# Result rows of the sorted products scattered to their tokens' places, and loaded in the third stage with plain transfers

## The reference

```
h  = concat(token_table[ids], cat_table[ids])                       # [64, 128, 256]
x1 = layernorm(h);  q, k, v = split(x1 @ W_qkv + b_qkv)              # 16 heads of 16
h  = h + linear_attention(elu(q) + 1, elu(k) + 1, v)                 # over each row of 128 tokens
x2 = layernorm(h)
rw = softmax over the experts with a positive gated logit of x2      # [tokens, 16]
q  = einsum('btc,ech,bte->bth', x2, q_proj, rw)   # and k, v likewise; 256 -> 128
ao = causal softmax(q k^T / sqrt(128)) v                             # over each row of 128 tokens
out = h + einsum('bth,ehc,bte->btc', ao, o_proj, rw)                 # 128 -> 256
```

## Time and profile before

| | us |
|---|---|
| median of three runs | 1116.49 |
| the profiled execution | 1116.51 |
| its span (first to last instruction) | 1114.8 |

### The profile page before, as it was taken

One profiled execution on the slowest core, in us unless ns is written; L12 is line 12 of the kernel. 1 busy time (PEld: TensorE's weight loads), 2 busy tenths in 40 slices (PEclk: granted clock), 3 DMA queues, 4 the chain that ended last, 5 costly groups with the idle time before them and its releaser, 6 DMA issues.

```text
span 1114.8 us, 23702 instructions
## 1 busy us (share of the span) xinstructions
PE 971.9 (87%) x6831; PEld 894.7 (80%) x6831; DVE 873.4 (78%) x2889; ACT 586.3 (53%) x1569; POOL 700.2 (63%) x924
## 2 busy tenths in 40 slices
PE   0788888878888872899999969999999999999998
PEld 0677777767777761889999859999999999999997
DVE  2578888788888875655555439999999999999998
ACT  1465666566566640444444435555555555555554
POOL 6667666566666667500000068888888888888885
PEclk9999999999999995999999969999999999999999
DMA  6464334433333324698888633333333333333331
GB/s 202 129 202 145 119 105 143 133 122 121 111 108 114 105 77 156 216 289 276 257 256 259 226 93 92 93 96 95 96 96 91 94 93 96 89 95 91 93 95 34
DMA packets 132325, 150.56 MB, mean 135 GB/s; under 512 B 14708, under 2 KB 119650, under 8 KB 132196
## 3 DMA queue, kind: packets, MB, share of 16 engines
q1 hardware_dynamic: 112964, 97.59, 28.2%
q0 software_dynamic: 18080, 50.36, 15.3%
q10 hardware_dynamic: 1152, 1.05, 0.3%
HBM read 83.79 MB, written 78.88 MB: 146 GB/s over the span
## 4 chain that ended last, share of the span: by engine, by line
PE 51%; DVE 24%; issue 9%; POOL 5%; DMA 4%; ACT 4%; SPq 1%; another core or an unknown queue 1%; POOLq 0%; DVEq 0%; ACTq 0%
PE bank L1429 11%; PE bank L1431 10%; PE bank L1430 10%; PE bank L1436 7%; PE bank L1460 5%; DVE w_attn L1412 5%; DVE qk_e L1366 3%; DVE row_x L1406 3%; DVE x L1366 3%; PE bank L1515 3%; DMA h<-in_L_tok_special_table,ids 2%; PE bank L1456 1%; ACT x L854 1%; PE bank L1631 1%; PE bank L1639 1%
## 5 line engine op out<-in xcount | busy, mean ns | idle before, releaser
L1429 PE MATMUL bank<-wo_hi,split_lo 128*128 128x256 f32 x1024 | 304.6, 297 | 10.0 <-DVE x L1366 4.4
L1431 PE MATMUL bank<-wo_hi,split_hi 128*128 128x256 f32 x1024 | 288.8, 282 | 0.0
L1430 PE MATMUL bank<-wo_lo,split_hi 128*128 128x256 f32 x1024 | 288.4, 282 | 0.0
L1429 PEld LDWEIGHTS bank<-wo_hi,split_lo 128*128 128x128 f32 x1024 | 194.0, 189 | 23.3 <-DVE qk_e L1366 11.2
L1430 PEld LDWEIGHTS bank<-wo_lo,split_hi 128*128 128x128 f32 x1024 | 194.2, 190 | 0.0
L1431 PEld LDWEIGHTS bank<-wo_hi,split_hi 128*128 128x128 f32 x1024 | 193.6, 189 | 0.0
L938 ACT ACTIVATE h<-bank,rwo 128x256 f32<-128x256 f32 x256 | 107.3, 470 | 115.2 <-PE bank L1431 111.4
L816 POOL DMA_INDIRECT row_y<-sorted_y,pair_now x128 | 124.1, 970 | 31.3 <-issue 21.3
L809 POOL COPY pair_now<-pair_at 128x2 uint32<-128x2 uint32 x64 | 11.7, 183 | 179.2 <-SPq L599 179.1
L1267 DVE TENSOR_TENSOR split_lo<-bank,split_hi 128x256 fp32r<-128x256 f32 x144 | 60.8, 422 | 68.7 <-ACT split_hi L900 67.4
L1366 DVE SCALAR_TENSOR_TENSOR qk_e<-bank,rwo,qk_e 128x256 f32<-128x256 f32 x256 | 108.6, 473 | 3.7 <-PE bank L1431 3.0
(11 more groups left out here) (228 smaller groups left out, 2675.4 us busy)
## 6 DMA issues: line engine op xcount, KB each, us to landing
sorted_y<-row_y SPq DMA_DIRECT2D x36, 384.0 KB, 3.1
sorted_y<-w_attn SPq DMA_DIRECT2D x36, 384.0 KB, 3.1
row_x<-sorted_x SPq DMA_DIRECT2D x72, 128.0 KB, 2.9
h_rows<-h SPq DMA_DIRECT2D x64, 128.0 KB
row_x<-h_rows SPq DMA_DIRECT2D x64, 128.0 KB, 2.2
out_h<-row_x SPq DMA_DIRECT2D x64, 128.0 KB, 1.7
embed_table<-in_L_tok_token_table SPq DMA_DIRECT2D x10, 625.0 KB
embed_table<-in_L_tok_special_table SPq DMA_DIRECT2D x10, 623.0 KB
```

The source lines that it names most:

```text
L1429: pe.matmul(ps, left[1][c], right[0][c], start=(c == 0), stop=False)
L1430: pe.matmul(ps, left[0][c], right[1][c], start=False, stop=False)
L1431: last = pe.matmul(ps, left[0][c], right[0][c], start=False, stop=(c == n - 1))
```

## The change

What is stored from the second stage isn't in sorted order any more. Each sorted row carries two marks behind its 256 values: its expert, and twice its token's number. So a row of `sorted_x` has 258 values (1032 bytes), and so have the buffers `x2` (12 now, 10 before), the zero rows and the loads of the second stage. Zero rows carry expert 0 and a token number beyond all tokens. For each pair tile VectorE forms the rows' destinations: twice the token number, plus one where the mark differs from the expert of the tile (the second choice of that token). GpSimd scatters each product to that row of `token_y`, 144 indirect DMAs with a bounds check that drops zero rows. The third stage loads a token tile's two rows of each token with one plain DMA from SyncE's queue, where GpSimd gathered them. The row arithmetic on GpSimd at the start of the second stage and three links of VectorE's table chain are gone.

```diff
@@ first stage: marks
+                slots = slice(first % N_X2, first % N_X2 + n)
+                dve.tensor_copy(marks[:, slots, C], top_at[:, tiles, 0])
...
                 for t in scatters_at(i.c):
-                    quad_done(pool, "position_index", group_of(t))
+                    g = group_of(t)
+                    first, n = GROUPS[g]
+                    quad_done(pool, "position_index", g)
+                    if t == first:
+                        slots = slice(first % N_X2, first % N_X2 + n)
+                        pool.tensor_copy(marks[:, slots, C + 1], token_twice[:, first:first + n]
+                                         ).then_inc(done["rows_marked"], 1)
+                    quad_done(pool, "rows_marked", g)
                     for n in range(2):
                         pool.indirect_dma_start(out=sorted_x, out_offset=offsets(position_u[:, t, n:n + 1]),
-                                                in_=x2[t % N_X2], in_offset=None
+                                                in_=x2_row[t % N_X2], in_offset=None
                                                 ).then_inc(scattered[t % N_X2], 16)
@@ second stage, SyncE
-                        after(sp, "pair_turned", tile.shift(-8))
+                        after(sp, "row_ids", tile.shift(-8))
                         sp.dma_start(x_buf[tile.c % 8], sorted_x[bass.ds(rows[tile.q], P), :]
                                      ).then_inc(pair_loaded[tile.c % 8], 16)
-                    tile = i.shift(-1)
-                    if tile.inside(PAIR_TILES) and tile.p:
-                        after(sp, "pair_copied", tile)
-                        first, buf = tile.shift(-1), y_buf[tile.c % 8 // 4]
-                        sp.dma_start(sorted_y[bass.ds(first.t * P, 2 * P), :].rearrange("(n p) y -> p n y", p=P),
-                                     buf[:, first.q:first.q + 2, :]).then_inc(y_stored[tile.c % 8 // 2], 16)
@@ second stage, GpSimd
-                for e in range(1, E):
-                    ...
-                    pool.tensor_scalar(term[e % 2], rows, float(e * REGION), y_step[:, e:e + 1],
-                                       ALU.is_ge, ALU.mult).then_inc(pairs_placed, 1)
-                    ...
-                    pool.tensor_tensor(total, rows if e == 1 else total, term[e % 2], ALU.add
-                                       ).then_inc(pairs_placed, 1)
+                both = token_y.rearrange("t (n y) -> (t n) y", n=2)
+                def step2(i):
+                    if i.inside(PAIR_TILES):
+                        after(pool, "pair_copied", i)
+                        after(pool, "row_ids", i)
+                        pool.indirect_dma_start(out=both, out_offset=offsets(row_ids[:, i.c:i.c + 1]),
+                                                in_=y_buf[i.c % 8], in_offset=None,
+                                                bounds_check=2 * B * T - 1, oob_is_err=False
+                                                ).then_inc(y_stored[i.c % 8], 16)
+                run2(pool, step2)
@@ second stage, VectorE: before its steps, and behind the low part of each tile
+                for g in range(2):
+                    last = dve.tensor_scalar(attn[:, g * P:(g + 1) * P], ident[:, :], tab[:, g, 0:1], None, ALU.mult)
...
+                dve.wait_ge(table_t, 4)
+                dve.tensor_copy(tile_expert, ps_x2[:, 0:2 * P]).then_inc(setup_v, 1)
...
+                        dve.scalar_tensor_tensor(row_ids[:, t:t + 1], x_buf[t % 8][:, C:C + 1], tile_expert[:, t:t + 1],
+                                                 x_buf[t % 8][:, C + 1:ROW], ALU.not_equal, ALU.add
+                                                 ).then_inc(done["row_ids"], 1)
@@ third stage, SyncE
+                tile = i.shift(4)
+                if tile.inside(B):
+                    after(sp, "qkv_sum", tile.shift(-2))
+                    sp.dma_start(y_all[:, 2 * tile.p * Y:2 * (tile.p + 1) * Y], token_y[bass.ds(tile.t * T, T), :]
+                                 ).then_inc(pairs_loaded[tile.p], 16)
@@ third stage, GpSimd
-                tile = i.shift(4)
-                if tile.inside(B):
-                    pool.tensor_copy(pair_now[tile.q][:, :], ...).then_inc(done["pair_picked"], 1)
-                    after(pool, "pair_picked", tile)
-                    after(pool, "qkv_sum", tile.shift(-2))
-                    take_wait()
-                    for n in range(2):
-                        pool.indirect_dma_start(out=row_y[:, 2 * tile.p + n, :], out_offset=None, in_=sorted_y,
-                                                in_offset=offsets(pair_now[tile.q][:, n:n + 1])
-                                                ).then_inc(pairs_gathered[tile.p], 16)
```

More of the change, by code:

```diff
@@ L245, in build @@
         y_flat = row_y[:, :, :].rearrange("p q y -> p (q y)")
-        x2 = [y_flat[:, n * C:(n + 1) * C] for n in range(4 * Y // C)]
-        x2 += [sb(f"x2_{n}", [P, C])[:, :] for n in range(len(x2), N_X2)]
+        x2_row = [y_all[:, n * ROW:(n + 1) * ROW] for n in range(N_X2)]
+        x2 = [b[:, 0:C] for b in x2_row]
+        marks = y_all[:, 0:N_X2 * ROW].rearrange("p (n r) -> p n r", r=ROW)
+        acc_b = sb("acc_b", [P, C])
+        row_ids = sb("row_ids", [P, PAIR_TILES], U32)
         h = [h4[:, q, :] for q in range(4)] + [row_x[:, q, :] for q in range(4)]
-        x_buf = [row_x[:, q, :] for q in range(4)] + [b[:, c * C:(c + 1) * C] for b in (phi, qk_neg) for c in range(2)]
-        y_buf = row_y, w_attn[:, :, :].rearrange("p c n -> p (c n)").rearrange("p (q y) -> p q y", y=Y)
+        x_buf = [x_all[:, n * ROW:(n + 1) * ROW] for n in range(8)]
+        y_buf = [y_all[:, n * Y:(n + 1) * Y] for n in range(8)]
+        tile_expert = vx[:, :, :].rearrange("p g n -> p (g n)")[:, 0:2 * P]
         qkv = [w_attn[:, :, :].rearrange("p c n -> p (c n)")[:, q * Y:(q + 1) * Y] for q in range(4)]
-        pair_now = [sb(f"pair_now{q}", [P, 2], U32) for q in range(4)]
         w_attn_s = [w[:, :, :].rearrange("p e c -> p (e c)")[:, 0:CH * 3 * C].rearrange("p (c n) -> p c n", c=CH)
@@ L442, in y_landed @@
             if tile.exists:
-                eng.wait_ge(y_stored[tile.c % 8 // 2], tile.eighth * 16 + 16)
+                eng.wait_ge(y_stored[tile.c % 8], tile.eighth * 16 + 16)
         def run1(eng, step):
@@ L604, in dense_way @@
                     load_weight(sp, 3 * E + e)
-                rest = sorted_y[B * P:PAIR_TILES * P, :].rearrange("r y -> (r y)").rearrange(
-                    "(n p c) -> n p c", p=P, c=C)
                 sp.wait_ge(routed, 1)
-                for n in range(rest.shape[0]):
-                    sp.dma_start(rest[n], zeros[:, :]).then_inc(y_filled, 16)
-                sp.wait_ge(y_filled, 16 * rest.shape[0])
+                for t in range(B):
+                    for lo, hi in ((Y, Y + C), (Y + C, 2 * Y)):
+                        sp.dma_start(token_y[t * T:(t + 1) * T, lo:hi], zeros[:, 0:hi - lo]).then_inc(y_filled, 16)
+                sp.wait_ge(y_filled, 16 * 2 * B)
                 def token_tile(t, first):
@@ L688, in _ @@
             pool.wait_ge(small_loaded, 64)
-            waits_taken = [0]
-            def take_wait():
-                n = waits_taken[0] % 8
-                waits_taken[0] += 1
-                pool.tensor_tensor(waiter[:, n:n + 1], ones[:, 0:1], ones[:, 0:1], ALU.add)
             def in_parts(tile):
@@ L964, in step3 @@
                 if tile.inside(B):
-                    landed_half(act, pairs_gathered, tile, dmas=2)
+                    landed_half(act, pairs_loaded, tile)
                     act.mul(qkv[tile.q][:, :], row_y[:, 2 * tile.p, :],
@@ L1546, in sorted_way @@
                 pe.wait_ge(weights_lo, 3 * E)
+                pe.wait_ge(setup_v, 8)
+                for g in range(2):
+                    last = pe.matmul(ps_x2[:, g * P:(g + 1) * P], ones[:, :], attn[:, g * P:(g + 1) * P], start=True,
+                                     stop=True)
+                last.then_inc(table_t, 1)
                 experts = {}
@@ L1559, in step2 @@
                         pe.wait_ge(pair_loaded[tile.c % 8], tile.eighth * 16 + 16)
-                        turn(ps_turn[tile.p], *halves(x_buf[tile.c % 8])).then_inc(done["pair_turned"], 1)
+                        turn(ps_turn[tile.p], *halves(x_buf[tile.c % 8][:, 0:C])).then_inc(done["pair_turned"], 1)
                     if i.inside(PAIR_TILES):
```

82 lines of the change are left out of this document (34 added, 48 removed).

## The result

The changed kernel takes 1169.87 us (median of 4 runs, 1166.12 to 1172.84); the kernel before, beside it, 1117.93 us (4 runs, 1114.16 to 1120.62). The ratio is 1.0465, with a 95% interval of 1.042 to 1.0511. The forecast was 1110.0, its range 1097 to 1126: wrong in sign and size.

The account below looks back on a forecast made before the run. TensorE was taken to bound stage two, and a chain of waits through VectorE, with a hidden GpSimd share, stage three. Terms +1.5 + 0 + 4.9 + 1.0 - 2.3 - 11.6 = -6.5 us took 1116.5 to 1110.0, range 1097 to 1126.

Parts of the forecast that it names:

- the backlog grows to 6 tiles only at the end, so TensorE isn't stopped: Stage two: copies wait for the scatter eight tiles before; GpSimd at 1.33 us against TensorE's 1.27 falls behind slowly, costing TensorE nothing.
- +4.9 and +1.0: Stage two: +4.9 us from scatters at 1.33 us each bounding the stage, +1.0 from `row_ids` work on VectorE at its start.
- TensorE was to be idle only near the end of the stage: Sign for stage two: TensorE has idle time only near the stage's end or none, with scatters spaced 1.33 us.
- Rival (c): Stage two: scatters cost over 1.33 us each; slower than before at 1.38, 1127 us in total at 1.45; chance 0.18.
- +13.5 at 1.39 us per scatter: Stage two: alternative to the +4.9 us term, should each scatter cost 1.39 us in place of 1.33.
- The loads of x, `row_ids`, 1032-byte rows: Stage two: later release of x loads costs nothing, `row_ids` +1.0 us, unaligned rows 0 up to 1.6 times their DMA time.
- rival d: Stage two: 1032-byte rows at twice the old cost make DMA engines set 1.48 us per tile, 1131 us; chance 0.05.
- First stage, +1.5: First stage: GpSimd's added copies and waits near the end +0.8 us, VectorE's 18 small copies +0.7.
- Start of the third stage, -2.3: Between last landing and first use of a row: 5.3 us becomes about 3 with a plain load; -2.3 us (0 to -4).
- 1 us to land: End of stage two: the last scatters, spare tiles with dropped rows, land 1 us after 645.5, at 646.5.
- Third stage, period 7.11 to 6.92 by the lock: Stage three: VectorE's two-input operations wait for GpSimd's adds at a shared port; the add starts 0.19 us earlier; -11.6 us in 61 tiles.
- the whole lock sequence shifts with it: Stage three: with add 801 starting 0.19 us earlier, 1406, add 803, 1412 and the next slot 1 all come 0.19 earlier.

Follow-up runs that it names:

- e8: Changed kernel, even tiles scattered to constant consecutive rows, odd tiles stored by GpSimd's plain transfers, permutation left out: 1108.4 us, kernel before 1115.5.
- e1: Changed kernel, second stage's products stored by SyncE's plain 384 KB transfers in sorted order, no scatters, permutation left out: 1088.7 us, kernel before 1085.5.
- e9: Kernel before, without GpSimd's index-column copy and tiny addition in stage three; gathers read pair_at directly: 1110.5 us against 1114.0, ratio 0.9967.
- e14: Kernel before plus 112 extra GpSimd scatters of 512 bytes per row in stage two, none at every eighth tile: 1150.1 us.
- e2: Kernel before plus 128 extra GpSimd scatters of 4 bytes per row in stage two: 1164.3 us, kernel before 1085.5.

## Why the prediction was wrong, by its own steps

**The step that failed: "the backlog grows to 6 tiles only at the end, so TensorE isn't stopped".** The sum of stage two held GpSimd's time per scatter (1.33 forecast, 1.29 measured) and nothing for what indirect transfers, one after another, do to the reports of TensorE: forecast +4.9 and +1.0, measured +59.5 (from 1.305 to 1.722 us per tile). The sign of it is one that the forecast named itself: TensorE was to be idle only near the end of the stage, and is busy 80.8 of 100 us in its middle. I looked at gathers four to a stretch and concluded nothing for 144 in a row. A sign of it may have lain in the trace of before: in the first stage, beside the x scatters, GpSimd waits up to 2.3 us for a small operation of VectorE that it waits at most 1.1 for on the chips where this stage is shorter. I had read that stage only for the price of a scatter.

**Rival (c), "the scatters cost more than 1.33 each"**, had the right place and the wrong mechanism; its 1.38 to 1.45 us never came. Its 1127 us was too mild, and my range had no term for a loss in other engines. (Its side figure, +13.5 at 1.39 us per scatter, comes to +13.3.)

**The loads of x, `row_ids`, 1032-byte rows (rival d).** Costed at nothing or 1 us, rightly: e8 has them all at 1.289 us per tile, with 0.83 DMA share. A packet of x takes 57.5 ns on average in e1, for 52.8 before: 9% more, far from the 1.6 times that would have been covered. `row_ids` takes 0.21 us.

**First stage, +1.5.** +1.8 in the pair of traces, but on chips of the long kind the eight traces with this first stage reach stage two at 442.5 to 453.6 us, and the six with that of before at 441.0 to 452.8, so a term of this size can't be read.

**Start of the third stage, -2.3.** Measured +1.6. The chain of waits of the changed kernel:
```profile
701.37 2.62 DMA token_y<-y_all,row_ids
...
704.23 2.75 issue
706.98 3.06 DMA y_all<-token_y
...
710.06 0.62 ACT y_all L947
```
The load takes the 3.06 us forecast, from issue to first use. The last scatter is 2.62 us in flight, where 1 us to land was put without a row for it. I also left out that a scatter first takes GpSimd's own time (copied at 700.10, in flight from 701.37; before, 638.49 and 639.00), and that 2.75 us pass in SyncE between the last landing and the load, across the branch and the hand-over.

**Third stage, period 7.11 to 6.92 by the lock.** Right in mechanism, about 0.6 of the size: 7.00, or -7.4 us in 63 periods for -11.6 forecast. One period of the chain in the changed kernel, to be laid beside the earlier trace rows:
```profile
781.35 0.56 DVE x_all L1396
781.91 1.01 DVE y_all L1402
782.92 0.39 DVE x L1356
783.32 0.40 DVE acc_b L1356
783.76 0.39 PE bank L1419
...
784.74 0.32 PE bank L1626 x2
...
787.40 0.13 PE bank L1421
787.62 0.34 issue
787.96 0.36 DVE qk_e L1356
788.35 0.56 DVE x_all L1396
```
and GpSimd, beside the earlier trace rows:
```profile
780.89 0.74 POOL L793 TENSOR_TENSOR x2T<-h,x2T 128x256 f32<-128x256 f32 x1 [2.65 <-ACT h L918]
781.71 0.80 POOL L795 TENSOR_TENSOR x2T<-h,x2T 128x256 f32<-128x256 f32 x1
```
The add now starts with ScalarE's hand-over (779.91 + 0.84 + 0.14 = 780.89), and line 1396 ends 0.28 us after the add, line 1402 0.41 after the next one: the lock sequence as forecast. In this period line 1396 takes 0.56 where 1406 took 0.74, the 0.18 gained. But from the end of the sum to the next start of 1396 it takes 788.35 - 782.92 = 5.43 us where it took 726.36 - 721.01 = 5.35: TensorE's part of this leg, from its first product (783.76, before 721.86) to its last (787.53, before 725.54), grew by 0.09 us; the pair of transposes in it takes 0.32 (line 1626, at 784.74) where it took 0.22 (line 1631, at 722.84). So in these two periods nearly half of the gain came back outside the lock, and "the whole lock sequence shifts with it" took that leg as fixed. One period doesn't stand for all, though: over tiles 8 to 55 line 1406 took 0.655 us on average, and under 0.5 in 13 of 48, with a longer leg behind it; line 1396 takes 0.562. On average this line became 0.09 us shorter and the leg 0.04 (5.456 to 5.416), and the line behind it 0.02 longer. What was mis-sized is the lock's own cost per tile, read from one period; why the short ones occur is open. e9 shows the cause of the gain apart from the change: with the gathers still on GpSimd, the freed add alone gives 0.06 of the 0.11 us.

## What to carry to other kernels

Indirect transfers of GpSimd issued in runs (of three or four in e14, of five in the changed kernel) can make the rest of the core slower though no engine and no DMA queue is full: look at how long after a matmul's end the engine that waits for it starts, and compare a stretch with such transfers against one without. Before moving them into a stage that TensorE fills, put dummy ones there (512 bytes a row, awaited by nobody): one run prices the move. A plain transfer in every second or third place ended the loss here; a slower TensorE did not. Ask which chip it ran on: on the two that ran the kernel before in 1085 to 1088 us, almost nothing was late (12 of 288 at most, in e2), but the full scatters never ran there.

## What I had not expected of the hardware

- Late reports, up to 4.7 us in the changed kernel, from TensorE to ScalarE and VectorE beside runs of indirect transfers, either direction, with 4 to 1536 bytes a row; 0.1 to 0.3 us at the median otherwise. Why, and what ends most of them 0.8 to 1.3 us after the last transfer of a run, is open.
- Scatters of 4 bytes a row filled the DMA engines (share 1.02 at 182 GB/s) and cost 79 us for 128 of them, in a single run.
- Chips differ: 1085 to 1088 or 1114 to 1116 us for the same kernel, all of it in the first stage, where the trace of the slower kind lacks over a quarter of the engines' semaphore updates.
- One more transpose of 32 rows cost TensorE more (1.59 us per tile) than one of 128 rows (1.38).
